# A relational graph network on one core: counts go through three PSUM banks in place of two, and six one-hots of a pair are made ahead of its additions

## What is computed

```python
h = relu(layernorm(x)); h = relu(h @ node_proj_w.T + node_proj_b)
for l in range(2):
    trans = einsum('nh,tdh->tnd', h, edge_W[l])       # 8 types
    msgs = trans[edge_type, src]                      # 100000 rows
    agg = segment_sum(msgs, dst, num_segments=6250)
    h = relu(gru_cell(agg, h, wih[l], whh[l], bih[l], bhh[l]))
out = x + h @ out_w.T + out_b
```

## Time and profile before

| | |
|---|---|
| median of 3 runs | 1701.7 us (1701.03 to 1707.34) |
| profiled execution, its own time | 1704.55 us |
| span of the profile | 1702.8 us |
| PE busy | 1472.4 us (86%) |
| POOL busy | 1198.4 us (70%) |
| DVE busy | 758.2 us (45%) |
| ACT busy | 544.9 us (32%) |
| mean granted TensorE clock | 0.953 of full |

### The profile page before, as it was taken

How to read it: one execution, slowest core, us unless ns; L and a number is a source line. 1 busy time by engine, 2 the same in 40 slices (tenths; PEclk the granted TensorE clock), 3 DMA queues, 4 the chain that set the end, 5 groups by cost and what they waited for, 6 DMA issues and landing times.

```text
span 1702.8 us, 34470 instructions
## 1 busy us (share of the span) xinstructions
PE 1472.4 (86%) x10602; PEld 1022.9 (60%) x10603; DVE 758.2 (45%) x3419; ACT 544.9 (32%) x1274; POOL 1198.4 (70%) x1258
## 2 busy tenths in 40 slices
PE   4668989899898886888875899999898888999997
PEld 2445556556555564777763566656565566788885
DVE  8777343342433236555545322322433334444454
ACT  4435162533516213333322111111625412222222
POOL 4667776667677677777772777777777777777772
PEclk9989999999999999999997999999999998899999
DMA  6623838457293433333332888886354374333331
GB/s 146 175 70 98 281 114 270 136 173 239 86 303 92 132 99 93 95 92 98 99 85 77 278 293 296 280 299 178 95 141 127 107 179 109 86 92 87 85 89 41
DMA packets 183378, 251.83 MB, mean 148 GB/s; under 512 B 24446, under 2 KB 156644, under 8 KB 183268
## 3 DMA queue, kind: packets, MB, share of 16 engines
q0 software_dynamic: 58368, 119.62, 25.5%
q1 hardware_dynamic: 123041, 130.73, 24.3%
q10 hardware_dynamic: 1858, 0.07, 0.1%
HBM read 212.20 MB, written 38.12 MB: 147 GB/s over the span
## 4 chain that ended last, share of the span: by engine, by line
PE 54%; DVE 10%; issue 10%; POOL 10%; DMA 8%; ACT 5%; DVEq 1%; POOLq 0%; ACTq 0%; SPq 0%; PEldq 0%
PE ps L988 12%; POOL gath L575 10%; PE ps L1058 9%; PE ps L965 7%; PE ps L927 6%; PE ps L1050 6%; PE ps L1038 5%; PE ps L1030 4%; DMA gath<-node_table,gidx 3%; DMA blocks<-node_table 3%; ACT counts L739 3%; DMA kept_counts<-counts 2%; PE ps L954 1%; DVE acc L1547 1%; PE ps L953 1%
## 5 line engine op out<-in xcount | busy, mean ns | idle before, releaser
L575 POOL DMA_INDIRECT gath<-node_table,gidx x1216 | 1161.6, 955 | 445.8 <-issue 354.1
L1547 DVE TENSOR_TENSOR acc<-ps,acc 128x16 f32 x864 | 150.0, 174 | 657.1 <-PE ps L1058 550.6
L988 PE MATMUL ps<-counts,blocks 128*128 128x504 f16 (+3 forms) x1764 | 387.7, 371 | 11.6 <-DMA blocks<-node_table 10.9
L785 ACT COPY sums_sb<-ps 128x512 f32<-128x512 f32 x216 | 126.5, 586 | 581.9 <-PE ps L1050 561.6
L988 PEld LDWEIGHTS ps<-counts,blocks 128*128 128x128 bf16 x1764 | 168.4, 98 | 182.2 <-DMA blocks<-node_table 18.1
L965 PE MATMUL ps<-work 128*128 128x392 bf16 x983 | 215.6, 332 | 68.9 <-ACT counts L739 39.7
L739 ACT CAST counts<-ps 128x392 f16<-128x392 f32 x429 | 198.0, 487 | 113.3 <-PE ps L965 97.6
L1058 PE MATMUL ps<-sums_sb,wT 128*128 128x128 f32 x1728 | 216.6, 279 | 9.5 <-ACT sums_sb L785 9.5
L1058 PEld LDWEIGHTS ps<-sums_sb,wT 128*128 128x128 f32 x1728 | 206.6, 194 | 17.9 <-DVE acc L1547 8.0
L1050 PE MATMUL ps<-onehot,gath 128*128 128x128 bf16 x2592 | 186.0, 224 | 36.2 <-DMA gath<-node_table,gidx 32.4
L1050 PEld LDWEIGHTS ps<-onehot,gath 128*128 128x128 bf16 x2592 | 165.6, 100 | 78.6 <-DMA gath<-node_table,gidx 39.4
(11 more groups left out here) (195 smaller groups left out, 906.3 us busy)
## 6 DMA issues: line engine op xcount, KB each, us to landing
blocks<-node_table SPq DMA_DIRECT2D x84, 672.0 KB
kept_counts<-counts SPq DMA_DIRECT2D x28, 882.0 KB
counts<-kept_counts SPq DMA_DIRECT2D x28, 882.0 KB, 7.7
gath<-node_table,gidx POOLq DMA_INDIRECT x1216
node_table<-gath SPq DMA_DIRECT2D x14, 336.0 KB, 2.8
node_table<-work SPq DMA_DIRECT2D x14, 336.0 KB, 2.9
counts<-in_x_dram SPq DMA_DIRECT2D x1, 3080.0 KB
out_dram<-counts SPq DMA_DIRECT2D x13, 224.0 KB, 2.7
```

What stands on the lines that cost most here:

```text
L575: nc.gpsimd.indirect_dma_start(out=gath[:, b, j, :], out_offset=None, in_=tables[l], in_offset=bass.IndirectOffsetOnAxis(ap=gidx[:, b, j:j ...
L785: act.copy(n_sb[:, b // 2, b % 2 * BG:(b % 2 + 1) * BG, :], narrow_sums[b % 2]) \
L988: last = nc.tensor.matmul(head_ps[:, 0:COLS[share]], blocks[:, j % 2, at, part * H:(part + 1) * H], counts[:, a, 0:COLS[share]], start=(i ...
L1547: nc.vector.tensor_tensor(win, narrow_ps[q][:, g * NARROW:(g + 1) * NARROW], win, ALU.add) \
```

## The change

Units are counted into banks 6, 7 and 3 in turn. PE waits before unit u for the copy of unit u - 3. Bank 3 is also the bank of the head's sums, so the first unit of a share that goes there waits until ACT has copied the sums of the share before (`head_copied`). And `add_narrow` makes the first six of its one-hots before its first wait and addition; the rest are spread over the eight additions as before.

```diff
--- before.py
+++ after.py
@@ -118,7 +118,9 @@
 
 
 
+
 SLOT_WORK, SLOT_UNITS, READ_PRODUCTS, PAIR_GROUPS, TYPE_WORK = 7900, 8, 16, 12, 4300
+FIRST_HOTS = 6
 BLOCKS = 7
 LOADS = HI // BLOCKS
 PRODUCTS = HI * PARTS
@@ -316,7 +318,7 @@
         own_r, own_in, own_hn, own_z = (ps[:, b, 0:TILE] for b in range(4))
         grows_ps = ps[0:ROWP, 6, :].rearrange("p (c h) -> p c h", c=TC)
 
-        unit_ps = [ps[:, 6 + b, 0:HICODES] for b in range(2)]
+        unit_ps = [ps[:, b, 0:HICODES] for b in (6, 7, 3)]
         spread_ps = ps[:, 6, 0:2 * HEAD].rearrange("p (a g) -> p a g", a=2)
         head_ps = ps[:, 3, 0:SHARE_UNITS * T]
         nodes_ps = ps[:, 1, 0:SHARE_UNITS]
@@ -735,8 +737,8 @@
                 at = (u - SHARE_FROM[share]) * T
                 if u == SHARE_TO[0] - 1:
                     for spare in range(COLS[0], SHARE_UNITS * T, T):
-                        act.copy(counts[:, :, spare:spare + T], unit_ps[u % 2].rearrange("p (a t) -> p a t", t=T))
-                act.copy(counts[:, :, at:at + T], unit_ps[u % 2].rearrange("p (a t) -> p a t", t=T)) \
+                        act.copy(counts[:, :, spare:spare + T], unit_ps[u % 3].rearrange("p (a t) -> p a t", t=T))
+                act.copy(counts[:, :, at:at + T], unit_ps[u % 3].rearrange("p (a t) -> p a t", t=T)) \
                    .then_inc(unit_copied, 1)
 
             def copy_head(l, share):
@@ -954,15 +956,17 @@
                         last = nc.tensor.matmul(grows_ps[:, c, :], ones_row[:, 0:ROWP], outb_row[:], start=False, stop=True)
                 last.then_inc(st[s]["turned"], 1)
 
-            def count_unit(u, share):
+            def count_unit(l, u, share):
 
                 k = UNITS[u][1]
                 pe.wait_ge(hots_lo_hi, COUNTED[u][-1] + 1)
-                if u > 1:
-                    pe.wait_ge(unit_copied, u - 1)
+                if u % 3 == 2 and u < SHARE_FROM[share] + 3 and turn_of(l, share) > 0:
+                    pe.wait_ge(head_copied, turn_of(l, share))
+                if u > 2:
+                    pe.wait_ge(unit_copied, u - 2)
                 for g in COUNTED[u]:
                     at = (LO_AT[g] + k - FROM[g]) * GE
-                    last = nc.tensor.matmul(unit_ps[u % 2], hot_lo[:, at:at + GE], hot_hi[:, g % HI_SPACE, :],
+                    last = nc.tensor.matmul(unit_ps[u % 3], hot_lo[:, at:at + GE], hot_hi[:, g % HI_SPACE, :],
                                             start=(g == COUNTED[u][0]), stop=(g == COUNTED[u][-1]))
                 last.then_inc(unit_ready, 1)
 
@@ -1009,7 +1013,7 @@
                 for kind, share, (lo, hi) in slot_of(l, i):
                     if kind == "count":
                         for u in range(lo, hi):
-                            count_unit(u, share)
+                            count_unit(l, u, share)
                     elif kind == "sum":
                         sum_head(l, share, lo, hi)
                     elif kind == "type":
@@ -1532,6 +1536,9 @@
                           .then_inc(sem_l["acc_added"], 1)
 
                 def add_narrow(k, g0, q, after_head, hots):
+                    for g in hots[:FIRST_HOTS]:
+                        make_hots(g)
+                    hots = hots[FIRST_HOTS:]
                     for half in range(2):
                         _, starts = nc.values_load_multi_w_load_instructions(
                             start_row[0:1, ds(g0 + half * BG, BG)], engines=(mybir.EngineType.DVE,), min_val=0, max_val=N,
```

## The result

The changed kernel takes 1689.87 us in the median of 9 runs (1685.61 to 1694.77), the kernel before 1708.84 in 9 runs on the same chips (1701.03 to 1714.6): a ratio of 0.9907, 95% interval 0.9885 to 0.9928. It is faster by 0.9%, where 1.7% was forecast, and the time lies at the range's upper end of 1690.

The account below looks back on a forecast made before the run. POOL's gathers were taken to set the pace. Against the profiled 1704.55 us: -28.5 (first head) - 2.5 (second layer) + 2 (slower gathers) = -29; from the median 1701.7 that gives 1673 us, range 1664 to 1690.

Parts of the forecast that it names:

- What bounds the kernel: Whole program: POOL's 1216 gathers set the pace, 1520 of 1604 us; only POOL's waits beyond that can go.
- What can go: POOL's waits before gathers: 28.5 us in the first layer's head, 2.5 us in the second layer's counts.
- the first wait: POOL's wait at 100.61 us, first layer's head: 4.33 us, said to stay because the change does not touch its cause.
- What the third bank gives PE: Counting slots, first head: a slot of 4.39 us takes about 3.24; PE saves some 30 us of waits for copies.
- the one-hots' terms: In the forecast's sum: +2 us for gathers slowed beside one-hots made back to back.
- What the six early one-hots give: First head: PE's waits for one-hots shrink by 8 us, at zero cost to the additions.
- The unknown price: Gathers beside one-hots made back to back, in 35 pairs: between nothing and 7 us, taken as 2 us.
- the bursts hold the gathers: Rival, chance 0.04: 35 bursts stretch three gathers each by 0.45 us, 47 us against 31, giving 1718 us.
- take PE's place: Rival, chance 0.17: ACT's copies hold the counting slots above 5.0 us; gain about 13 us, 1688 us (1682 to 1693).
- The end did give: Rival, chance 0.06: the second layer's last rounds also lose 2.8 us of waits; 1664 to 1668 us.
- The clock rival: Rival, chance 0.05: PE's waits for gathers lower its clock in the first head, costing 17 us; 1682 to 1687 us.
- The other marks for being wrong: POOL's waits above 15 us from 90 to 616 us, or waits gone there that return before 921 us.

Follow-up runs that it names:

- e2: The changed kernel with two banks again, its six early one-hots kept; time within half a per cent of the kernel before (1706.98 us on that chip).
- e10: One edit of the changed kernel, with three banks; the text does not say which edit or its time (kernel before on that chip: 1703.82 us).
- e8: The changed kernel without early one-hots (FIRST_HOTS = 0), the third bank alone, second run of this edit; 1667.6 us.
- The run with pieces: The changed kernel with its early one-hots made in pieces of 128 and 98 columns; 1710.1 us.
- the spaced run: The changed kernel with VectorE waiting for its own one-hots behind each early pair; 14.6 us of the median come back against the change.
- every other column: The changed kernel with each early pair's high one-hot reading every other column of its table; longest gather 4.37 us, median time not in the text.

## Why the prediction was right and wrong

**What bounds the kernel**: right. In all twelve kernels the time of the profiled run, less the gathers' sum and their idle time, is 97.2 to 99.7 us, while the time itself goes from 1667 to 1710.

**What can go**: right, and a little small. The idle time before the gathers fell by 37.3 us where 31 were counted: 29.0 in the first head (28.5 forecast), 4.2 in the second layer's counts (2.5 forecast), 3.2 behind them, where I had expected nothing, and 0.9 from 921 to 1198 us. Of this, 5.4 us stood under "issue" (354.1 to 348.7), where the profile names no releaser. The first head's gain would have been 2 us larger but for the first wait, which was said to stay at 4.33 us and came out at 6.4. What differs there is PE's start, by 0.9 us, and TensorE's clock. In before the granted clock rises from the lower level, 1.2 GHz, to the upper, 2.4 GHz, at about 98.4 us (0.82 from 98 to 99, 1.00 from 99 on), in the change at about 102.2 (0.50 until 102), after the same slot of 11 matmuls behind the long wait for one-hots. The 24 matmuls in front of the types, before and then after:

```profile
98.08 1.64 PE L1050 MATMUL ps<-onehot,gath 128*128 128x128 bf16 x24
```

```profile
99.05 2.77 PE L1054 MATMUL ps<-onehot,gath 128*128 128x128 bf16 x24
```

In e2 and e10 the clock rises near 98.4 us too, and the wait is 4.3; in the other eight it rises at 100.2 to 102.5, and the wait is 6.3 us or more. Both kernels with two banks are of the early kind, and of the ten with three banks only e10 is; what decides, and whether the third bank has a part in it, stays open.

**What the third bank gives PE**: right. The slot takes 3.23 us (3.24 forecast), the waits for copies are 5.0 us (under 10), and PE waits for gathers. Alone it gives a ratio of 0.9783, where the sum without the one-hots' terms, -31 us, would have made it 0.982.

**What the six early one-hots give**: right in the trace, and worth nothing beside the third bank. PE's waits for one-hots went from 18.3 to 9.7 us, but the third bank alone had already taken away all that POOL waited for. I had added both savings into one sum for PE (30 + 8 - 1.5) to cover 28.5 us of waits, and had not asked what the 30 give alone. They suffice: the idle time in the first head is 124.9 us in e8 and 124.6 in the change. Then the second part of the change could only cost.

**The unknown price**: here the prediction failed. The step is the term of +2 us for "a gather beside one-hots made back to back", put between 0 and 7; it is 21.1 us. The other terms of the sum gave more than forecast, and this one took it back. Two readings led there. The upper end rested on the first 14 groups as the densest case, "the longest of all 1216" gathers beside them with 1.40 us. They are as dense, but their low one-hots are 128 to 256 columns wide and take 0.25 to 0.28 us, while those of the burst shown are 512 to 768 wide and take 0.34 to 0.41. The run with pieces shows that length matters, though by itself it is not enough. And "twelve that were spread were already almost as dense" took busy share for what matters: between them stand additions that wait on semaphores, and the spaced run shows that such a wait is what lets a gather in.

**The rival "the bursts hold the gathers"** (0.04) was the mechanism that acted, with the wrong shape: 0.45 us on each of three gathers. In truth one gather takes most or all of a burst, up to 2.9 us above its 0.95, and most bursts stretch no other; and not every burst holds one. The 0.45 us that I gave it for a gather was no bound: no stretch of before had six pairs of long one-hots back to back.

**The other rivals.** ACT did not take PE's place: 22 waits of POOL at 0.3 us each. The waits that went did not return later in the first layer. The end did give, 3.2 us of idle time from 1345 us on, but the gathers there took 2.1 us more. The clock rival acted in part, without a cost that any run shows. Between 430 and 450 us the granted clock was 1.00, where the earlier trace rows had 0.84, but from 90 to 218 us it was 0.91 against 0.95, over the whole first head 0.96 against 0.98, and over the program 0.938 against 0.953. Behind 103 us of the first head it stood at its lower level for 27 us, against 14 before, and five of its six falls in the change come beside a wait of PE for a gather of 3.4 to 5.5 us, the sixth beside one of 2.1 (waits of 2.3 and 3.1 us at 475 and 558 us brought none). The argument that waits for gathers leave the clock at 1.00 did not carry over from the stretch from 1020 to 1198 us, where PE's waits for them were of at most 1.4 us. Since POOL sets the pace, PE has the time to lose: with the third bank alone the clock is 0.97 in the first head, and 0.940 and 0.951 over the program, and those are the fastest kernels.

**The mark that was missed**: the text says that a median above 0.96 us would show the gathers held. The median is 0.946 or 0.947 in all the kernels. Thirteen gathers in 1216 carry the loss, so only the sum or the maximum shows it. The other marks for being wrong stayed silent too. The mark that did speak is the last gather, at 1657.9 us where 1645 was forecast; with the third bank alone it is at 1639.4 and 1634.6.

## What to carry to other kernels

When GpSimd's gathers set the pace, read how VectorE's instructions stand beside them: long one-source instructions that read at an even step, one behind the other with no semaphore between, can hold a gather until the last of them ends. Spread them among work that waits, or leave a wait between them. (Cut short they let the gathers in as well, but here that made VectorE late and cost more than it gave, 1710.1 us.) Give a ring that drains one more buffer first and measure that alone: if it lifts the pace-setter's waits entirely, a second edit for the same waits has nothing to win. And when a price is bounded by the worst case seen, check that this case has the size of what is coming as well as its density.

## What the runs showed that was not expected

A burst need not hold a gather. In the change, some bursts of twelve let all of them through, and in this one VectorE pays instead:

```profile
327.53 0.50 DVE L1416 TENSOR_SCALAR work<-iota_h,lo_place 128x768 bf16<-128x768 f16 x1
...
328.15 0.95 POOL L577 DMA_INDIRECT gath<-node_table,gidx  x1 [0.30 <-issue]
...
328.73 0.58 DVE L1416 TENSOR_SCALAR work<-iota_h,lo_place 128x896 bf16<-128x896 f16 x1
...
329.40 0.95 POOL L577 DMA_INDIRECT gath<-node_table,gidx  x1 [0.30 <-issue]
...
329.95 0.59 DVE L1416 TENSOR_SCALAR work<-iota_h,lo_place 128x768 bf16<-128x768 f16 x1
```

Behind the start of each of three gathers one instruction of VectorE is longer by 0.1 to 0.2 us (0.50 and 0.59 where 768 columns take 0.41, 0.58 where 896 take 0.45), and this burst lasts 3.79 us instead of 3.0 to 3.3; some of that is its wider one-hots. The burst from 239.35 us holds no gather and lasts 3.23, so there nobody pays. Of the first head's bursts, those from 133.34, 149.38, 163.68, 247.00 and 255.66 us hold a gather almost to their end or beyond it, those from 239.35, 327.53 and 427.14, of twelve too, hold none, and others stretch one in part. What decides stays open: a gather that starts 0.47 us before the burst can be held too (255.19, 3.86 us), and one that starts 0.45 us before another is not (426.69, 1.01 us). So the loss may vary with small shifts of time. The spread of the runs does not show it: it is 9 us in the change, 22 with every other column, and 14 in the kernel before, which holds no gather. A single bad gather in a trace is no accident to be set aside.
